# Cross-attention and a mixture of experts on one core: routing moved forward, copies laid out by rank, and the last sums split between TensorE and VectorE

## The chip, the cores and the metric

The kernel runs on one core of a Trainium2 chip. The time is the device time of the whole kernel in microseconds. The kernel before took 362.15 us as the median of 3 runs (361.63 to 363.35). Engines are called TensorE (PE), VectorE (DVE), ScalarE (ACT), GpSimd (POOL) and SyncE (SP).

## The reference

8 batches of 112 tokens with 256 features (896 tokens). First cross-attention with 16 heads over 375 context rows, then a mixture of 32 experts, of which each token uses 4, and a shared expert:

```
x = x + relu(attention(layernorm(x), ctx) @ wo.T + wo_b)
scores = softmax(xf @ gw + gb)              # xf = layernorm(x), 896 x 256; scores 896 x 32
keep the 4 best of 8 groups (by their two best experts), then the 4 best experts of these
y = sum over the 4 experts of weight * ((silu(xf@w1+b1) * (xf@w3+b3)) @ w2 + b2)
z = (silu(xf@sw1+sb1) * (xf@sw3+sb3)) @ sw2 + sb2
x = x + y + z
```

All of it is float32.

## The kernel before

The program has two blocks of instructions, `attention` and `experts`; at the end of the first all engines wait for each other.

**Attention** goes through 32 groups of four heads. At its end VectorE normalises the tokens of batches 0 to 6 (`normalise`, semaphore `xn_ok`), TensorE turns the last sums and projects batch 7, and VectorE normalises batch 7. TensorE fills waits with matmuls whose result nobody reads (`warm`, line 301).

**Routing** (start of `experts`): TensorE transposes the 896 normalised tokens (line 808), ScalarE and VectorE copy them to `xf`, TensorE makes the logits (line 816), and VectorE takes them through softmax, choice of groups and choice of experts (`choose`, `sel`). Every step of that row on VectorE waits for the one before (`chained`). Between the steps VectorE closes the shared expert's halves (`shared_h`, line 972), whose matmuls (`shared_up`, line 827) TensorE runs meanwhile. From `sel`, matmuls with `earlier` and `ones` count how many tokens chose an expert before each token and in all (lines 839 to 846). From these VectorE works out the place (slot) of each of the 3584 copies: each expert's copies lie together, in whole blocks of 128 rows. There are always 59 blocks; those that no expert needs come last.

**Scatter**: when `slots_ok` is given, GpSimd issues 32 indirect DMAs (line 794, `expert_rows<-normed,slots`) that write the rows of one batch each, rank 3 of all batches first, rank 0 last. Rank 0 of a token is its highest slot. SyncE loads block j (line 755, 128 KB) for j under 4 only when rank 3-j is scattered, so block 3 waits for all 32. Beside it VectorE makes a table of which expert owns each block, on one partition (lines 1062 to 1072), the weights of the copies (`gate`, lines 1075 to 1078), and adds the shared expert's result to `x2` (line 1082).

**Expert loop**: for each block TensorE transposes the rows (`turn_rows`, line 870), multiplies by the block's expert's w1 and w3 (`up`, line 878), transposes the product of silu and the other half (`turn_h`, line 887) and multiplies by w2 (`down`, line 893). VectorE adds biases (line 1106), multiplies (line 1112) and copies the result (`copy_y`, line 1088); ScalarE copies transposes and takes silu. GpSimd scatters each block's 128 results to `ys` in HBM (line 799, `expert_out<-hs,to`). Where each goes is worked out from marks read back from the blocks (`marks`, line 764; `results_go`, line 1095, called at j = 5), in time for the first of these scatters.

**Sums**: in `ys` the four copies of a token lie side by side. When all 59 scatters have landed, SyncE loads 8 batches of 448 KB (line 768, `b<-expert_out`), VectorE adds four weighted rows per batch to `x2` (line 1119), and SyncE writes each batch out (line 773). The buffer `rows` is the one of the biases, `b13`.

## Time and profile before

| What | Value |
|---|---|
| median of 3 runs | 362.15 us |
| profiled execution: its own time, its span | 361.01 us, 359.2 us |
| attention block | 0 to about 160 us |
| routing up to the first scatter | 160 to 186.8 us |
| 32 scatters up to block 3 in SBUF | 186.8 to 232.4 us |
| expert loop | up to 332.3 us |
| last result scatter landed | 337.1 us |
| loads, sums and stores | 337.1 to 359.2 us |
| busy share of PE, DVE, ACT, POOL | 81%, 62%, 42%, 51% |

The span is the time from the first to the last record of the profile; the time of the execution is a little longer. Busy shares are means over the whole span, so they say little of the stretches in which the engines wait for each other: those are read from the chain of waits and from the timeline.

### The profile page before, as it was taken

The numbers are of one execution on the slowest core, as the hardware profiler recorded it, in microseconds if no ns is written. First come the engines' busy times: TensorE is split into PE (matmuls) and PEld (weight loads), VectorE is DVE, ScalarE is ACT, GpSimd is POOL, SyncE is SP. The second block draws the span as 40 slices with busy tenths as digits, with TensorE's granted clock in tenths as the row PEclk, the third lists the DMA queues.
The fourth block names the chain that finished last, engine by engine and source line by source line (L and its number), as shares of the span: only waits on it lengthen the run. The fifth ranks groups of instructions, "written<-read, shape, count | busy, mean of one in ns | idle before, by whom it ended". The sixth has DMA issues, their size and how long they took to land.

```text
span 359.2 us, 7134 instructions
## 1 busy us (share of the span) xinstructions
PE 290.2 (81%) x2301; PEld 202.9 (56%) x2301; DVE 222.8 (62%) x708; ACT 150.9 (42%) x403; POOL 181.7 (51%) x188
## 2 busy tenths in 40 slices
PE   8999999999999999899898022199999999999000
PEld 3466666666666667656474011077778777776000
DVE  1678877767777778276969200065666666656097
ACT  1267666666566666515110000044545545544000
POOL 7266757565657566110027777307556555556200
PEclk9999999999999999999999555589999999999655
DMA  6795888959794900009502333385555455542495
GB/s 150 206 78 149 261 240 244 265 172 292 218 326 138 308 5 2 2 13 295 162 0 79 109 110 114 116 101 161 162 167 157 148 167 158 155 154 76 159 242 168
DMA packets 54013, 55.92 MB, mean 156 GB/s; under 512 B 18925, under 2 KB 45562, under 8 KB 53466
## 3 DMA queue, kind: packets, MB, share of 16 engines
q1 hardware_dynamic: 49610, 43.94, 45.6%
q0 software_dynamic: 4368, 11.52, 9.8%
q8 instruction: 21, 0.34, 0.4%
q14 instruction: 14, 0.11, 0.1%
HBM read 35.03 MB, written 20.41 MB: 154 GB/s over the span
## 4 chain that ended last, share of the span: by engine, by line
PE 29%; DVE 9%; POOL 9%; issue 4%; DMA 3%; ACT 0%; POOLq 0%; DVEq 0%; SPq 0%
PE ps L878 14%; POOL expert_rows L794 9%; PE ps L893 7%; DVE x L1119 4%; PE ps L870 3%; PE ps L887 2%; DMA b<-expert_out 1%; PE ps L816 1%; DMA expert_rows<-normed,slots 1%; DMA expert_out<-hs,to 1%; DMA xg<-expert_rows 1%; POOL expert_out L799 1%; PE ps L846 1%; PE ps L808 0%; PE ps L841 0%
## 5 line engine op out<-in xcount | busy, mean ns | idle before, releaser
L289 POOL TENSOR_SCALAR z<-z,zmax 112x375 f32<-112x375 f32 x64 | 78.7, 1241 | 52.7 <-DVE zmax L555 52.7
L799 POOL DMA_INDIRECT expert_out<-hs,to x59 | 56.6, 959 | 50.3 <-DVE hs L1088 35.2
L555 DVE CUSTOM_DVE_ANT_0 z<-ps,mask_sb 112x375 f32<-112x375 f32 x128 | 62.5, 546 | 28.8 <-PE ps L368 28.8
L483 ACT ACTIVATE pT<-ps 125x336 f32<-125x336 f32 x128 | 50.7, 448 | 38.1 <-PE ps L345 37.7
L878 PE MATMUL ps<-w,xgT 128*128 x236 | 64.1, 396 | 0.0
L345 PE MATMUL ps<-ident,z 112*125 112x112 f32 x384 | 56.6, 283 | 0.2 <-ACT pT L483 0.2
L345 PEld LDWEIGHTS ps<-ident,z 112*125 112x125 f32 x384 | 47.3, 188 | 15.4 <-ACT pT L483 7.3
L1106 DVE TENSOR_TENSOR hb<-ps,b 128x256 f32<-128x256 f32 x59 | 25.1, 425 | 49.1 <-PE ps L878 49.1
L794 POOL DMA_INDIRECT expert_rows<-normed,slots x32 | 32.4, 1014 | 35.1 <-DVE normed L1059 25.7
L878 PEld LDWEIGHTS ps<-w,xgT 128*128 128x128 f32 x236 | 43.5, 196 | 10.0 <-issue 1.8
L870 PE MATMUL ps<-ident,xg 128*128 128x128 f32 x118 | 24.0, 287 | 30.2 <-DMA xg<-expert_rows 30.2
L935 ACT COPY xgT<-ps 128x256 f32<-128x256 f32 x59 | 22.0, 373 | 46.4 <-PE ps L870 46.4
L893 PE MATMUL ps<-w2s,hs 128*128 x118 | 36.0, 387 | 0.0
L942 ACT COPY hs<-ps 128x128 f32<-128x128 f32 x59 | 15.7, 266 | 47.8 <-PE ps L887 47.8
L870 PEld LDWEIGHTS ps<-ident,xg 128*128 128x128 f32 x118 | 14.8, 146 | 33.2 <-DMA xg<-expert_rows 25.9
L1112 DVE TENSOR_TENSOR hh<-hb,sg 128x128 f32<-128x128 f32 x59 | 17.3, 293 | 19.5 <-ACT sg L947 17.0
L368 PE MATMUL ps<-kT,qT 32*112 32x375 f32 x256 | 28.8, 519 | 0.0
L381 PE MATMUL ps<-pT,vaug 125*32 125x112 f32 x768 | 25.0, 263 | 0.6 <-ACT pT L483 0.6
L1088 DVE COPY hs<-ps 128x256 f32<-128x256 f32 x59 | 24.5, 415 | 1.1 <-PE ps L893 0.6
L301 PE MATMUL ps<-ident 128*128 128x512 f32 x44 | 23.6, 669 | 1.6 <-POOL ident L256 1.6
L565 DVE TENSOR_SCALAR z<-z,zmax 112x375 f32<-112x375 f32 x32 | 23.7, 741 | 0.0
L1119 DVE SCALAR_TENSOR_TENSOR x<-b,gate,x 112x256 f32<-112x256 f32 x32 | 14.9, 484 | 8.9 <-DMA b<-expert_out 8.1
(159 smaller groups left out, 348.8 us busy)
## 6 DMA issues: line engine op xcount, KB each, us to landing
xg<-expert_rows SPq DMA_DIRECT2D x59, 128.0 KB, 2.3
expert_rows<-zero SPq DMA_DIRECT2D x14, 512.0 KB, 10.0
w2s<-in_L_ffn_w SPq DMA_DIRECT2D x2, 2048.0 KB, 9.6
b<-in_L_ffn_b SPq DMA_DIRECT2D x2, 2048.0 KB, 14.1
b<-expert_out SPq DMA_DIRECT2D x8, 448.0 KB, 9.3
ctx_sb<-in_ctx SPq DMA_DIRECT2D x8, 375.0 KB
mask_sb<-in_mask_Bx1xSxS_ff SPq DMA_DIRECT2D x8, 164.1 KB, 2.4
expert_out<-hs,to POOLq DMA_INDIRECT x59, 2.8
```

The lines of the kernel that those rows point to most:

```text
L289: pool.tensor_scalar(z[:, n % RING, :], z[:, n % RING, :], zmax[:, n % RING:n % RING + 1], None, ALU.subtract).then_inc(by_pool, 1)
L345: ins = nc.tensor.transpose(bank[0:KP, c * S:(c + 1) * S], z[:, n % RING, c * KP:(c + 1) * KP], ident[0:S, 0:S])
L368: nc.tensor.matmul(ps[0:S, S_BANK + j, 0:SK], qT[rows, b % 2, g // 2, g % 2, :], kT[rows, b % 2, g // 2, :], start=True, stop=True).then_i ...
L483: nc.scalar.activation(pT[:, n % RING, :], ps[0:KP, T_BANK + at % 2, 0:KT * S], ACT.Exp).then_inc(ring_read, 1)
L555: nc.vector.tensor_tensor_reduce(out=z[:, n % RING, :], in0=ps[0:S, S_BANK + j, 0:SK], in1=mask_sb[:, b % 2, :], scale=-1.0 if j in ACT_HE ...
L794: pool.indirect_dma_start(xs, bass.IndirectOffsetOnAxis(ap=slots[:, b, r:r + 1], axis=0), normed[:, b, :], None).then_inc(scattered[r], 16)
L799: pool.indirect_dma_start(ys, bass.IndirectOffsetOnAxis(ap=to[:, j:j + 1], axis=0), y_sb[:, j % 4, :], None).then_inc(y_sent[j % 4], 16)
L870: ins = nc.tensor.transpose(ps[:, T_BANKS[j % 2], k * P:(k + 1) * P], xg[:, j % 4, k * P:(k + 1) * P], ident[:])
L878: ins = nc.tensor.matmul(ps[:, U_BANKS[j % 2], 0:2 * INTER], xgT[:, j % 4, k, :], w13[:, k, bass.ds(owner_of(words, j), 1), :].rearrange(" ...
L893: nc.tensor.matmul(ps[:, Y_BANKS[j % 2], 0:D], hT[:, j % 4, :], w2s[:, bass.ds(owner_of(words, j), 1), :].rearrange("p o c -> p (o c)"), s ...
L1106: TT(hb[:, j % 2, :], ps[:, U_BANKS[j % 2], 0:2 * INTER], b13[:, bass.ds(owner_of(words, j), 1), :].rearrange("p o c -> p (o c)"), ALU.add ...
L1119: ins = nc.vector.scalar_tensor_tensor(x2[:, b, :], rows[:, TOPK * b + r, :], gate[:, b, r:r + 1], x2[:, b, :], ALU.mult, ALU.add)
```

## The change

- Transposes and logits of batches 0 to 6 go from `experts` to the end of `attention`, in place of four filling matmuls; ScalarE does the copies. Batch 7 follows in `experts`.
- `ones`, `earlier` and `sel` are of type float32r, so the counting matmuls are in that type.
- `shared_h` 0 and 1 come after `sel`, 2 and 3 after the slots; `shared_up` 2 and 3 come after the counting.
- The unused blocks come first instead of last (`free`). The table of owners is made with one block per partition and packed by one matmul. `gate` is made in the expert loop, one operation per block from j = 10.
- In the first three blocks `turn_rows` runs one block ahead instead of two, and `down(0)` stands ahead of `turn_rows(3)`.
- `ys` is ordered by rank and then token. Rank r of a token has at least r blocks behind it, so rank 3 is loaded when blocks up to 55 have landed, rank 2 up to 56, rank 1 up to 57, and rank 0 when all have.
- Batches 0 to 3 are summed by VectorE. For batches 4 to 7 ScalarE makes 16 diagonal matrices of the weights in the loop (from j = 23), and TensorE sums with them in PSUM, with filling matmuls between; ScalarE copies the sums to `x2`.

```diff
+    SHARES = (4, 2, 2, 2)
...
+        LOGITS = SUM_BANK
+        def route(pe, b):
+            for k in range(DK):
+                ins = nc.tensor.matmul(ps[0:S, LOGITS, b * E:(b + 1) * E], xf[:, k, b * S:(b + 1) * S],
+                                       gw_sb[:, k, :], start=(k == 0), stop=(k == DK - 1))
+            return ins
...
-                pool.iota(tag_i[:], [[TOPK * S, B]], base=0, channel_multiplier=TOPK).then_inc(places, 1)
+                pool.iota(tag_i[:], [[S, B]], base=0, channel_multiplier=1).then_inc(places, 1)
...
-                warm(4, S_BANK)
+                for c, own_batches in ((0, range(0, B // 2)), (1, range(B // 2, B - 1))):
+                    pe.wait_ge(xn_ok, own_batches.stop)
+                    for k in range(DK):
+                        for b in own_batches:
+                            at = (b - own_batches.start) * S
+                            ins = nc.tensor.transpose(ps[:, 2 * c + k, at:at + S], normed[:, b, k * P:(k + 1) * P], ident[0:S, 0:S])
+                        ins.then_inc(xT_full, 1)
+                pe.wait_ge(sums_ok, B)
+                for b in range(B - 1):
+                    if b in (0, B // 2):
+                        pe.wait_ge(xf_by_act, 2 if b == 0 else 4)
+                    route(pe, b)
...
+                for n, (lo, hi, k) in enumerate(((0, B // 2, 0), (0, B // 2, 1), (B // 2, B - 1, 0), (B // 2, B - 1, 1))):
+                    act.wait_ge(xT_full, n + 1)
+                    nc.scalar.copy(xf[:, k, lo * S:hi * S], ps[:, n, 0:(hi - lo) * S]).then_inc(xf_by_act, 1)
                 roots(B - 1, B, 4)
...
-            ones = sbe("ones", [S, P])
-            earlier = sbe("earlier", [S, S])
+            ones = sbe("ones", [S, P], F32R)
+            earlier = sbe("earlier", [S, S], F32R)
...
-            sel = sbe("sel", [S, B, E])
+            sel = sbe("sel", [S, B, E], F32R)
...
+            BY_DVE, BY_PE = range(0, B // 2), range(B // 2, B)
+            diag = xf[0:S].rearrange("p k c -> p (k c)").rearrange("p (n s) -> p n s", s=S)
...
+            GATES_AT = 10
+            DIAG_AT = GATES_AT + 3 * TOPK + 1
+            def next_rows(j):
+                if j < TOPK - 2:
+                    return range(j + 1, j + 2)
+                if j == TOPK - 2:
+                    return range(j + 1, j + 3)
+                return range(j + 2, min(j + 3, NBLK))
...
+                sp.wait_ge(hs_ok, 2 * NSH)
...
+                for r in reversed(range(TOPK)):
+                    for q in range(4):
+                        sp.wait_ge(y_sent[q], 16 * len(range(q, NBLK - r, 4)))
+                    wide = B // SHARES[r]
+                    for c in range(SHARES[r]):
+                        sp.dma_start(rows[:, r * B + c * wide:r * B + (c + 1) * wide, :],
+                                     ys[r * T + c * wide * S:r * T + (c + 1) * wide * S, :].rearrange("(b s) d -> s b d", s=S)
+                                     ).then_inc(rows_in[r][c], 16)
                 for b in range(B):
-                    sp.dma_start(rows[:, TOPK * b:TOPK * (b + 1), :].rearrange("s r d -> s (r d)"),
...
-                    sp.wait_ge(summed, b + 1)
+                    if b in BY_DVE:
+                        sp.wait_ge(summed, (TOPK - 1) * len(BY_DVE) + b + 1)
+                    else:
+                        sp.wait_ge(moved, b - BY_PE.start + 1)
                     sp.dma_start(out[b], x2[:, b, :]).then_inc(out_sent, 16)
...
+                b = B - 1
+                pe.wait_ge(xn_ok, B)
+                for k in range(DK):
+                    ins = nc.tensor.transpose(ps[:, 5, k * S:(k + 1) * S], normed[:, b, k * P:(k + 1) * P], ident[0:S, 0:S])
+                ins.then_inc(xT_full, 1)
+                pe.wait_ge(xf_by_act, 5)
+                route(pe, b).then_inc(logits_ok, 1)
...
-                for u in range(2 * NSH):
+                for u in range(2):
                     shared_up(u)
...
+                for u in range(2, 2 * NSH):
+                    shared_up(u)
...
+                    if b == 1:
+                        pe.wait_ge(owner_ok, 1)
+                        nc.tensor.matmul(ps[0:1, 6, P:P + NWORD], owner[:], pack[:], start=True, stop=True).then_inc(words_full, 1)
...
-                turn_rows(1)
...
-                    if j + 2 < NBLK:
-                        turn_rows(j + 2)
-                    if j >= 2:
+                    if j == TOPK - 2:
                         down(j - 2)
+                    for n in next_rows(j):
+                        turn_rows(n)
+                    if j >= 2 and j != TOPK - 2:
+                        down(j - 2)
+                def fill(n):
+                    for _ in range(n):
+                        nc.tensor.matmul(ps[:, H_BANK, :].rearrange("p (r c) -> p r c", c=P), ident[:],
+                                         ident[:].unsqueeze(1).to_broadcast([P, BANK // P, P]), start=True, stop=True)
+                pe.wait_ge(hT_ok, NBLK)
+                pe.wait_ge(xgT_ok, NBLK)
+                pe.wait_ge(biased, NBLK)
+                pe.wait_ge(diag_ok, len(BY_PE) * TOPK)
+                for b in BY_PE:
+                    nc.tensor.matmul(ps[0:S, b, 0:D], ident[0:S, 0:S], x2[:, b, :], start=True, stop=False)
+                fill(3)
+                for r in reversed(range(TOPK)):
+                    for b in BY_PE:
+                        pe.wait_ge(rows_in[r][b * SHARES[r] // B], 16)
+                        nc.tensor.matmul(ps[0:S, b, 0:D], diag[:, (b - BY_PE.start) * TOPK + r, :],
+                                         rows[:, r * B + b, :], start=False, stop=(r == 0)).then_inc(added, 1)
+                    if r > 0:
+                        fill(1)
...
+                act.wait_ge(xT_full, 5)
+                nc.scalar.copy(xf[:, :, (B - 1) * S:B * S], ps[:, 5, 0:DK * S].rearrange("p (k s) -> p k s", k=DK)).then_inc(xf_by_act, 1)
...
+                def turn_weights(n):
+                    act.wait_ge(gates_ok, n % TOPK + 1)
+                    nc.scalar.activation(diag[:, n, :], ident[0:S, 0:S], ACT.Copy,
+                                         scale=gate[:, BY_PE.start + n // TOPK, n % TOPK:n % TOPK + 1]).then_inc(diag_ok, 1)
...
+                    if DIAG_AT <= j < DIAG_AT + len(BY_PE) * TOPK:
+                        turn_weights(j - DIAG_AT)
+                for b in BY_PE:
+                    act.wait_ge(added, len(BY_PE) * (TOPK - 1) + b - BY_PE.start + 1)
+                    nc.scalar.copy(x2[:, b, :], ps[0:S, b, 0:D]).then_inc(moved, 1)
...
+                apart = mine[:].rearrange("s b e -> s (b e)")[0:4 * NWORD, 0:4 * NWORD].rearrange("p (n f) -> p n f", f=4)
+                chained(TT(apart, ident[0:4 * NWORD, 0:4 * NWORD].rearrange("p (n f) -> p n f", f=4),
+                           places5[0:4 * NWORD].unsqueeze(1).to_broadcast([4 * NWORD, NWORD, 4]), ALU.mult))
+                chained(nc.vector.tensor_reduce(pack[:], apart, AX.X, ALU.add))
...
-                shared_h(0)
...
-                shared_h(1)
...
-                TT(cw[:, :, 0:E], sc[:], sel[:], ALU.mult).then_inc(cw_ok, 1)
-                shared_h(2)
-                shared_h(3)
+                TT(cw[:, :, 0:E], sc[:], sel[:].bitcast(F32), ALU.mult).then_inc(cw_ok, 1)
+                shared_h(0)
+                shared_h(1)
...
+                chained(nc.vector.tensor_scalar(free[:], ends[:, E - 1:E], -1.0, float(NBLK), ALU.mult, ALU.add))
+                chained(nc.vector.tensor_scalar(ends[:], ends[:], free[:], None, ALU.add))
...
-                for lo in range(0, 4 * NWORD, STEP):
...
-                    chained(nc.vector.tensor_reduce(gate[:, :, r], mine[:], AX.X, ALU.add))
+                chained(nc.vector.tensor_scalar(passed[:], ends[0:4 * NWORD], slot[0:4 * NWORD, 0:1], None, ALU.is_le))
+                chained(nc.vector.tensor_reduce(owner[:], passed[:], AX.X, ALU.add))
+                nc.vector.tensor_scalar(owner[:], owner[:], float(E - 1), None, ALU.min).then_inc(owner_ok, 1)
+                shared_h(2)
+                shared_h(3)
+                dve.wait_ge(words_full, 1)
+                nc.vector.tensor_copy(word_i[:], ps[0:1, 6, P:P + NWORD]).then_inc(table_ok, 1)
+                dve.wait_ge(table_ok, 1)
+                words = [dve.value_load(word_i[0:1, n:n + 1], min_val=0, max_val=E ** 4 - 1) for n in range(NWORD)]
...
+                def weigh_copies(n):
+                    r = n // 3
+                    if n % 3 == 0:
+                        chained(TT(mine[:], key[:], best[:, :, r:r + 1].to_broadcast([S, B, E]), ALU.is_equal))
+                    elif n % 3 == 1:
+                        chained(TT(mine[:], mine[:], cw[:, :, 0:E], ALU.mult))
+                    else:
+                        nc.vector.tensor_reduce(gate[:, :, r], mine[:], AX.X, ALU.add).then_inc(gates_ok, 1)
...
+                    if GATES_AT <= j < GATES_AT + 3 * TOPK:
+                        weigh_copies(j - GATES_AT)
...
-                for b in range(B):
...
-                    ins.then_inc(summed, 1)
+                dve.wait_ge(acc_ok, B)
+                dve.wait_ge(gates_ok, TOPK)
+                for n, r in enumerate(reversed(range(TOPK))):
+                    for b in BY_DVE:
+                        dve.wait_ge(rows_in[r][b * SHARES[r] // B], 16)
+                        if n:
+                            dve.wait_ge(summed, (n - 1) * len(BY_DVE) + b + 1)
+                        nc.vector.scalar_tensor_tensor(x2[:, b, :], rows[:, r * B + b, :], gate[:, b, r:r + 1],
+                                                       x2[:, b, :], ALU.mult, ALU.add).then_inc(summed, 1)
```

## Rows read from the trace of the kernel before

**Rows 1.** Chain of waits, whole span: shares by line.

```profile
by line: PE ps L878 13.7%; POOL expert_rows L794 8.8%; PE ps L893 6.7%; DVE x L1119 4.2%; issue 3.7%; PE ps L870 3.5%; PE ps L887 2.1%; DMA b<-expert_out 1.1%; PE ps L816 0.9%; DMA expert_rows<-normed,slots 0.7%; DMA expert_out<-hs,to 0.7%;
```

**Rows 2.** Timeline, attention to experts: start, duration (us), what, idle before.

```profile
154.68 2.35 DVE L544 TENSOR_SCALAR normed<-x,mv,rstd 112x256 f32<-112x256 f32 x7
156.08 3.60 PE L301 MATMUL ps<-ident 128*128 128x512 f32 x8
...
159.94 0.31 POOL L778 MEMSET restart<- 112x256 f32 x1 [14.68 <-POOLq L1125]
...
160.59 0.54 ACT L919 COPY xf<-ps 128x448 f32<-128x448 f32 x1 [1.66 <-PE ps L808]
```

**Rows 3.** Chain of waits, routing: start, duration (us), what.

```profile
159.98 1.72 PE ps L808 x16
161.75 3.32 PE ps L816 x32
165.16 0.43 DVE lg L985
...
172.01 0.68 DVE hs L972
...
177.98 0.43 DVE sel L1023
...
182.68 0.40 DVE over L1045
...
186.76 1.85 POOL expert_rows L794
...
191.05 0.94 POOL expert_rows L794
```

**Rows 4.** Stretches of 0.5 us: busy time of each engine, clock, DMA.

```profile
198.00:198.50 0.50, 0.00 (x0) 0.00 (x0) 0.50 (x3) 0.00 (x0) 0.50 (x1) 0.62 0.72 224
...
235.50:236.00 0.50, 0.50 (x4) 0.42 (x3) 0.12 (x1) 0.43 (x2) 0.00 (x0) 0.84 1.22 67
```

**Rows 5.** Chain of waits, last scatter and load of block 3.

```profile
227.71 2.58 DMA expert_rows<-normed,slots
230.30 2.07 DMA xg<-expert_rows
```

**Rows 6.** Timeline of the loop, and one DMA issue (KB, us to landing).

```profile
232.51 0.38 SPq L764 DMA_DIRECT2D marks<-expert_rows  x1
...
239.82 0.40 DVE L1095 TENSOR_TENSOR own_copy<-marks,slot 128x236 f32<-128x236 f32 x1
...
241.66 0.98 POOL L799 DMA_INDIRECT expert_out<-hs,to  x1 [13.02 <-DVE to L1098]
...
252.96 0.42 DVE L1106 TENSOR_TENSOR hb<-ps,b 128x256 f32<-128x256 f32 x1 [0.48 <-PE ps L878]
...
marks<-expert_rows SPq DMA_DIRECT2D x1, 236.0 KB, 6.5
```

**Rows 7.** Chain of waits, end of the kernel.

```profile
330.78 0.96 POOL expert_out L799
...
334.57 2.39 DMA expert_out<-hs,to
337.11 4.02 DMA b<-expert_out
...
356.44 0.48 DVE x L1119
```

**Rows 8.** Stretches: PE, PEld, DVE, ACT, POOL busy; clock, DMA share, GB/s.

```profile
4.00:8.00 4.00, 4.00 (x7) 1.64 (x6) 0.58 (x2) 0.05 (x1) 3.44 (x3) 1.00 1.02 241
100.00:105.00 5.00, 4.58 (x54) 3.23 (x54) 4.00 (x13) 3.58 (x9) 2.62 (x3) 1.00 1.04 331
...
339.00:343.00 4.00, 0.00 (x0) 0.00 (x0) 1.74 (x4) 0.00 (x0) 0.00 (x0) 0.50 0.96 278
343.00:350.00 7.00, 0.00 (x0) 0.00 (x0) 6.64 (x15) 0.00 (x0) 0.00 (x0) 0.50 1.04 238
```

More of the change, by code:

```diff
@@ L9 @@
 F32 = mybir.dt.float32
+F32R = mybir.dt.float32r
 U32 = mybir.dt.uint32
@@ L156, in xattn_moe_kernel @@
         xn_ok = sem("xn_ok")
+        xT_full = sem("xT_full")
+        xf_by_act = sem("xf_by_act")
+        logits_ok = sem("logits_ok")
         zero_ok = sem("zero_ok")
@@ L672, in xattn_moe_kernel @@
         y_sent = [sem(f"y_sent{q}") for q in range(4)]
-        rows_in = [sem(f"rows_in{b}") for b in range(B)]
+        gates_ok = sem("gates_ok")
+        diag_ok = sem("diag_ok")
+        added = sem("added")
+        moved = sem("moved")
+        rows_in = [[sem(f"rows_in{r}_{c}") for c in range(SHARES[r])] for r in range(TOPK)]
         summed = sem("summed")
@@ L711, in experts @@
             ends = sbe("ends", [P, E])
+            free = sbe("free", [P, 1])
             base1 = sbe("base1", [P, E])
@@ L735, in experts @@
             rows = b13[0:S]
+            ones1 = above[:].rearrange("s b e -> s (b e)")[:, 0:P]
+            earlier1 = above[:].rearrange("s b e -> s (b e)")[:, P:P + S]
             sil = xg[:].rearrange("p q d -> p (q d)")[:, 0:2 * CT].rearrange("p (u c) -> p u c", u=2)
@@ L780, in _ @@
                 pool.memset(cw[:], 1.0).then_inc(const_ok, 1)
-                pool.memset(ones[:], 1.0).then_inc(ones_ok2, 1)
+                pool.memset(ones1[:], 1.0).then_inc(ones_ok2, 1)
                 pool.wait_ge(const_ok, 3)
@@ L785, in _ @@
                 pool.wait_ge(ones_ok2, 1)
-                pool.affine_select(out=earlier[:], in_=ones[:, 0:S], compare_op=ALU.is_gt, fill=0.0, base=0,
+                pool.affine_select(out=earlier1[:], in_=ones1[:, 0:S], compare_op=ALU.is_gt, fill=0.0, base=0,
                                    pattern=[[1, S]], channel_multiplier=-1).then_inc(ones_ok2, 1)
+                pool.tensor_copy(ones[:], ones1[:]).then_inc(ones_ok2, 1)
+                pool.wait_ge(ones_ok2, 3)
+                pool.tensor_copy(earlier[:], earlier1[:]).then_inc(ones_ok2, 1)
                 pool.wait_ge(slots_ok, 2)
@@ L962, in over_e @@
                     return ap.unsqueeze(2).to_broadcast(shape)
-                for c in range(NCH):
-                    dve.wait_ge(xT_full, DK * c + 2)
-                    nc.vector.tensor_copy(xf[:, 1, c * CT:(c + 1) * CT], ps[:, DK * c + 1, 0:CT]).then_inc(xf_by_dve, 1)
                 def shared_h(u):
@@ L1053, in _ @@
                            base1[0:S].unsqueeze(1).to_broadcast([S, B, E]), ALU.add))
-                chained(TT(key[:], key[:], sel[:], ALU.mult))
+                chained(TT(key[:], key[:], sel[:].bitcast(F32), ALU.mult))
                 for b in range(B):
@@ L1059, in _ @@
                 nc.vector.tensor_scalar(normed[:, :, D:D + TOPK], best[:, :, 0:TOPK], -1.0, None, ALU.add).then_inc(slots_ok, 1)
-                for lo in range(0, 4 * NWORD, STEP):
-                    some = slice(lo, min(lo + STEP, 4 * NWORD))
-                    n = some.stop - lo
-                    passed = xf[0:1].rearrange("p k c -> p (k c)")[:, 0:n * E].rearrange("p (j e) -> p j e", e=E)
-                    chained(TT(passed, ends[0:1].unsqueeze(1).to_broadcast([1, n, E]),
-                               count1[0:1, some].unsqueeze(2).to_broadcast([1, n, E]), ALU.is_lt))
-                    chained(nc.vector.tensor_reduce(owner[:].rearrange("p n f -> p (n f)")[:, some], passed, AX.X, ALU.add))
-                chained(nc.vector.scalar_tensor_tensor(owner[:], owner[:], float(E - 1),
-                                                       places5[:].unsqueeze(1).to_broadcast([1, NWORD, 4]), ALU.min, ALU.mult))
-                chained(nc.vector.tensor_reduce(word[:], owner[:], AX.X, ALU.add))
-                nc.vector.tensor_copy(word_i[:], word[:]).then_inc(table_ok, 1)
-                for r in range(TOPK):
-                    chained(TT(mine[:], key[:], best[:, :, r:r + 1].to_broadcast([S, B, E]), ALU.is_equal))
-                    chained(TT(mine[:], mine[:], cw[:, :, 0:E], ALU.mult))
-                    chained(nc.vector.tensor_reduce(gate[:, :, r], mine[:], AX.X, ALU.add))
+                chained(nc.vector.tensor_scalar(passed[:], ends[0:4 * NWORD], slot[0:4 * NWORD, 0:1], None, ALU.is_le))
[7 more added lines that the diff above has]
+                words = [dve.value_load(word_i[0:1, n:n + 1], min_val=0, max_val=E ** 4 - 1) for n in range(NWORD)]
                 for b in range(B):
@@ L1112, in _ @@
                         TT(hh[:, j % 2, :], hb[:, j % 2, INTER:2 * INTER], sg[:, j % 2, :], ALU.mult).then_inc(h_ok, 1)
-                for b in range(B):
-                    dve.wait_ge(rows_in[b], 16)
-                    if b == 0:
-                        dve.wait_ge(acc_ok, B)
-                    for r in range(TOPK):
-                        ins = nc.vector.scalar_tensor_tensor(x2[:, b, :], rows[:, TOPK * b + r, :], gate[:, b, r:r + 1],
-                                                             x2[:, b, :], ALU.mult, ALU.add)
-                        if r < TOPK - 1:
-                            chained(ins)
-                    ins.then_inc(summed, 1)
+                dve.wait_ge(acc_ok, B)
[7 more added lines that the diff above has]
+                                                       x2[:, b, :], ALU.mult, ALU.add).then_inc(summed, 1)
         with ExitStack() as own_tiles:
```

61 lines of the change are left out of this document (20 added, 41 removed).

## The prediction, made before the changed kernel was run

> **What bounds the kernel now.** I read the page first: no engine bounds all of it. The chain of waits by line [rows 1] then splits the end of the kernel: the expert loop is a chain of TensorE lines (878, 893, 870, 887), but POOL's scatter of the rows (794) holds 8.8% and VectorE's last sums (1119) 4.2%. In order of time there are four links. Routing runs from 159.94, when both blocks' engines have met, to the first scatter at 186.76 [rows 2, 3], nearly all of it single VectorE steps behind each other. The scatter: 32 indirect DMAs up to 227.71, 2.58 to landing, 2.07 for block 3's load [rows 5]; blocks 0 to 2 are worked in its shadow. The loop, about 1.67 us a block. The end: last result scatter at 334.57, landed 337.11, first sum four us later, last sum at 356.44, span 359.2 [rows 7]. So a change helps only if it brings forward the first scatter, shortens the 32, or shortens what follows the last blocks. I call T3 the landing of the last row scatter (230.30) and TL that of the last result scatter (337.11).
>
> **Routing.** *Logits.* Normalised rows of batches 0 to 6 are complete at 154.68 + 2.35 = 157.03, while TensorE runs filling matmuls from 156.08 to 159.68 [rows 2]. In their place: transposes at 1.72/16 = 0.107 each (14: 1.5), four ScalarE copies of about 0.54 or less, one behind the other, and 28 of 32 logit matmul instructions at 3.32/32 = 0.104 [rows 2, 3]. First transposes 156.1, copies 156.7 to 158.8, logits of batches 0 to 3 at 158.0 to 159.65, of 4 to 6 to 160.95. The four filling matmuls hid this up to 159.68; beyond that it delays the meeting of the engines by 1.3, to 161.25. Then batch 7 alone: transposes and copy about 0.75, four matmul instructions 0.4, hand-overs 0.4, so VectorE begins line 985 at 162.8 instead of 165.16 [rows 3]: 2.35 less. VectorE's preparation, now with two more steps, ends about 162.7 and just fits. POOL's two extra copies lie in the same time. Bounds: 1.0 (the ScalarE copies late) to 3.5.
>
> *shared_h 0 and 1* stood in the chain as 172.01 and its twin; each delayed the next step by 0.6 [rows 3]. Off: 1.2.
>
> *Counting.* From the end of sel (178.41) to line 1045 (182.68) are 4.27 [rows 3] for 32 matmul instructions at the full clock. No row shows the price of float32r; a float32 product here is two instructions, so I count one in its place, 16 instead of 32 for lines 841 and 846. But TensorE is now idle before them: two shared_up end near 169, sel comes at 174.9. In the trace the granted clock fell from 2.4 to 1.2 GHz at 198.2, after TensorE had gone idle at 196.5, and came back to 2.4 at 235.6, over 3 us after work had begun again [rows 4]. So half as many at twice the duration: nothing gained, bounds 2.0 less (they stay at 2.4 GHz) and 2.0 more (float32r is no cheaper by instruction, all at 1.2 GHz). VectorE has shared_h 0 and 1 in this time.
>
> *free* adds two chained steps of about 0.2: 0.4 more. The first scatter comes 2.35 + 1.2 + 0 - 0.4 = 3.1 earlier, at 183.6.
>
> **Scatter.** The first two took 1.85, while VectorE made the table in four operations of over a microsecond on one partition; from 191.05 on they took 0.94 [rows 3]. The weights' operations beside the next five made them about 1.05. Both go away: the table is three small operations, and the weights move to the loop. 1.8 + 0.5 = 2.3 off. Lower bound 0.5, if the first two were slow because they were first. The Trainium skill ("SBUF — State Buffer", "Who interferes with whom") says that GpSimd and VectorE lock a port pair against each other when VectorE has two SBUF inputs while GpSimd reads SBUF. By that rule the weights' and the compare operations cost what they cost, and shared_h 2 and 3 and the additions to x2, with one input in PSUM, cost nothing: the same 2.3. The 0.94 of scatters beside the additions agrees.
>
> TensorE's shared work now partly follows the counting: two shared_up (6), eight batches (13), done by about 201; block 3 is needed after 224.9. Hidden. T3 moves 3.1 + 2.3 = 5.4, to 224.9.
>
> **Start of the loop.** After T3 TensorE had up(2), turn_h(1) and down(0) still to do; now they are done before. That is worth some 2 us: up(3) could start at T3 + 3.5 instead of T3 + 5.6. But results_go at j = 5 needs the marks, issued at T3 + 2.2 and landing 6.5 later, T3 + 8.7. Its first operation ran at 239.82 = T3 + 9.5, and hb(5) waited for its four operations [rows 6]. So the marks' landing becomes the bound after 0.8 us: I take 0.6 less. Bounds 0 and 2.
>
> **In the loop.** 12 operations of 0.42 on VectorE, one a block, each ahead of hb. VectorE sat idle 0.48 before hb [rows 6]: they fit barely; with 0.05 for the wait each, I allow 0.3 in all. If that cover is missed by half an operation in each block: 12 x 0.2 = 2.4. The 16 diagonals on ScalarE, about 0.3 each, stand behind silu, where ScalarE next waits 0.7 or more for turn_h: nothing. If they were late, 16 x 0.3 = 4.8. Empty blocks first instead of last changes no count; the last blocks' results now go to scattered rows like those of the middle: nothing. POOL's loop scatters have slack.
>
> **The end.** Before, from TL to the end of the span: 359.2 - 337.11 = 22.1, VectorE's 32 operations running without a pause once the first load was there. Now: the result scatters run 1.27 apart at the end (330.78 to 334.57 for three) [rows 7], so block 55 has landed about TL - 3.5, and rank 3 starts then; the others follow as their blocks land, and DMA always has work. To move: 3.67 MB and the last three scatters' 0.39, 4.06 MB. The rate: 278 GB/s beside VectorE alone, 238 with stores in the traffic (packets of 4 KB); rows of 1 KB on 112 partitions moved at 241 early in the kernel, those on 128 with stores at 331 [rows 8]. I take 270, near the row without stores, since the stores now come last: 15.0. With 2 for the first and last latency: TL - 3.5 + 17.0 = TL + 13.5. Behind the last landing: TensorE's two products 0.9 (its filling and products should keep it at 2.4 GHz), ScalarE's copy 0.4, hand-overs 0.4, and the last store as now, 359.2 - 356.92 = 2.3 [rows 7]: 4.0. VectorE's half (16 operations, 7.8) runs in step with the loads and is done before. End TL + 17.5 instead of TL + 22.1: 4.6 less. By 241 it is 2.7 less, by 331 it is 7.3 less.
>
> The Trainium skill ("DMA: Bandwidth & Descriptors", "Anatomy of one DMA") gives 2.0 us and then 436 GB/s for a DMA; that would be an estimate of 9.3 for the 4.06 MB, and a total some 6 us below mine. The rows of the tail contradict it: its DMA share was 0.96 to 1.04 at 238 to 278 GB/s.
>
> **Sum.** 5.4 + 0.6 - 0.3 + 4.6 = 10.3. Profiled execution 361.01 - 10.3 = 350.7; the median of the runs lies 1.14 above that execution, so 351.8.
>
> **Rivals.**
> 1. *The forecast*: routing 3, scatter 2, end 4 to 5. 346.5 to 356. Chance 0.66.
> 2. *The scatters were slow for being first, and the loads run at 241*: gain 3.1 + 0.5 + 0.6 - 0.3 + 2.7 = 6.6, time 355.6. For: the very first two, at 241 GB/s a row of like shape. Against: later ones also slowed under VectorE's weights. 0.14.
> 3. *Counting at 2.4 GHz or cheap at 1.2, loads at 300 or more*: 2 more and 2.7 more, 347.1. For: 331 at 100 us. Against: 238 in the tail itself; an idle gap of 6 before counting. 0.13.
> 4. *The loop's pace breaks*: VectorE's and ScalarE's added operations come late (2.4 + 4.8) : gain 3.4, 358.8. For: the 0.48 is thin. Against: ScalarE's slack. 0.04.
> 5. *Slower*: the loads of 1 KB packets into the buffer go at under half the rate. The front's 5.7 less is lost when the tail grows by 5.7: TL + 27.8 = -3.5 + 2 + 4.0 + 4.06/rate, a rate of 160 GB/s. At 120 the tail ends at TL + 36.3, 14.2 later, and the time is 370.7. Against: no stretch with 1 KB packets and a full DMA share was that slow. 0.03. That the sums could stay on VectorE's pace is excluded by the code, which gives it half.
>
> Less than 0.5% (1.8 us) is about what a measurement of this kernel can tell from no change. Faster takes rivals 1 to 4 but for the upper edge of 4 and of misses that add up: 0.95; within 0.02; slower 0.03. The range, 346.0 to 356.6, holds the forecast's span and most of rivals 2 and 3; the rest is some 0.15.
>
> **What would show it.** In the profile after: the engines meet at 161.2 and line 985's successor starts near 162.8; the first scatter near 183.6 and of 0.94 to 1.0; a granted clock of half in the counting; the last row scatter landed near 225; marks bind results_go; blocks still 1.67 apart from j = 10 to 38; loads of rank 3 issued 3.5 before the last landing, the last load landed 13.5 after it, and 4 from there to the end. A first scatter later than 185, scatters of 1.85 again, a wait of TensorE for hh in j = 10 to 21, or loads that end 16 or more after TL would make the forecast wrong.

## The result, and the profile after

The changed kernel took 351.58 us (median of 4 runs, 351.42 to 351.92) against 362.02 for the kernel before (4 runs), a ratio of 0.972 with a 95% interval of 0.968 to 0.975. Run again later (run 9), beside 11 runs of the kernel before, it took 352.79 against 361.41, a ratio of 0.977 (0.975 to 0.978). So the gain is 8.6 to 10.4 us. The two profiled executions stand 9.09 apart (361.01 and 351.92, the span of the latter 350.1), and the terms below are of these two. The executions of the changed kernel differ among themselves by 0.5 us here and by 2.4 in run 9, so a term of a few tenths is a reading of two traces and no proof by itself; the logits, `shared_h` and the order ahead of block 3 were not tried alone.

Chain of waits of the changed kernel, routing (start, duration, what), to be laid beside [rows 2, 3]; logits are L1087, the counting L897 to L904:

```profile
162.97 0.44 DVE lg L1087
...
174.62 0.44 DVE sel L1125
...
175.10 0.56 PE ps L897
175.65 1.15 PE ps L899 x7
176.80 1.72 PE ps L904 x8
...
178.54 0.40 DVE over L1146
...
179.81 0.16 DVE free L1152
...
183.08 1.16 POOL expert_rows L859
```

Of the page, the busy shares of the engines and the chain by line; before they were 81%, 62%, 42% and 51%, and [rows 1]:

```profile
PE 308.0 (88%) x2331; PEld 212.3 (61%) x2331; DVE 209.9 (60%) x691; ACT 158.1 (45%) x426; POOL 179.8 (51%) x190
...
PE ps L941 13%; POOL expert_rows L859 8%; PE ps L956 6%; PE ps L933 3%; DMA b<-expert_out 3%; PE ps L950 2%; DMA expert_out<-hs,to 1%; PE ps L996 1%; DMA expert_rows<-normed,slots 1%; DMA xg<-expert_rows 1%; POOL expert_out L864 1%; DVE hb L1214 1%; PE ps L904 0%; DVE best L1108 0%; ACT sg L1030 0%
```

VectorE's last sums (4.2% before) are gone from the chain; transfers of results (`b<-expert_out`, 3%) and TensorE's products with the diagonal matrices (L996, 1%) stand there instead. The first scatter starts 3.7 earlier than before (186.76). The chain of waits again, from the last row scatter into the loop ([rows 5, 6]). L941 is `up`, here of block 3; `hh` is the product behind it on VectorE, and `own_copy` the first of the four operations that need the marks:

```profile
221.92 2.56 DMA expert_rows<-normed,slots
224.50 2.04 DMA xg<-expert_rows
...
226.58 1.29 PE ps L933 x4
...
228.01 2.07 PE ps L941 x4
...
233.48 0.29 DVE hh L1220
233.77 0.33 DVE own_copy L1201
```

Stretches (PE, PEld, DVE, ACT, POOL busy; granted clock, DMA share, GB/s), first around the counting, then in the tail ([rows 4, 8]):

```profile
172.50:173.00 0.50, 0.00 (x0) 0.00 (x0) 0.47 (x3) 0.00 (x0) 0.00 (x0) 0.72 1.08 295
...
175.00:178.00 3.00, 2.90 (x15) 2.90 (x15) 1.65 (x4) 0.00 (x0) 0.00 (x0) 0.50 0.68 194
...
230.50:231.00 0.50, 0.50 (x4) 0.47 (x3) 0.50 (x2) 0.34 (x2) 0.00 (x0) 0.75 1.52 82
...
330.00:332.00 2.00, 1.19 (x3) 0.19 (x1) 0.00 (x0) 0.00 (x0) 0.07 (x1) 1.00 1.01 336
...
336.00:338.00 2.00, 1.24 (x4) 0.38 (x2) 1.32 (x4) 0.00 (x0) 0.00 (x0) 1.00 1.12 238
```

Chain of waits at the end ([rows 7]); the last result scatter is issued at 329.12 (334.57 before):

```profile
327.86 4.79 DMA expert_out<-hs,to
...
333.04 9.47 DMA b<-expert_out
342.56 1.98 PE ps L996 x8
...
345.40 1.83 PE ps L996 x8
347.25 0.37 ACT x L1048
```

Laid side by side, the 9.1 us are (the landing of the last row scatter itself took 2.6 in both):

| stretch | before | after | gain | forecast |
|---|---|---|---|---|
| first scatter starts | 186.76 | 183.08 | 3.7 | 3.1 |
| first to last row scatter | 40.95 | 38.84 | 2.1 | 2.3 |
| landing of the last to first result scatter | 11.36 | 11.05 | 0.3 | 0.6 |
| first to last result scatter | 92.91 | 93.59 | -0.7 | -0.3 |
| last result scatter issued to end of span | 24.63 | 20.98 | 3.7 | 4.6 |

### The profile page after: what moved, and what is told of

It reads as the page before. It is cut to its first block, busy times and chain, and to the rows that moved or that the text cites. A ratio compares the mean times of both kernels' runs of the same rounds, so it can differ in the third digit from the quotient of the medians.

```text
span 350.1 us, 7231 instructions
## 1 busy us (share of the span) xinstructions
PE 308.0 (88%) x2331; PEld 212.3 (61%) x2331; DVE 209.9 (60%) x691; ACT 158.1 (45%) x426; POOL 179.8 (51%) x190
## 4 chain that ended last, share of the span: by engine, by line
PE 27%; POOL 9%; DVE 6%; DMA 5%; issue 4%; ACT 1%; DVEq 0%; SPq 0%; POOLq 0%
PE ps L941 13%; POOL expert_rows L859 8%; PE ps L956 6%; PE ps L933 3%; DMA b<-expert_out 3%; PE ps L950 2%; DMA expert_out<-hs,to 1%; PE ps L996 1%; DMA expert_rows<-normed,slots 1%; DMA xg<-expert_rows 1%; POOL expert_out L864 1%; DVE hb L1214 1%; PE ps L904 0%; DVE best L1108 0%; ACT sg L1030 0%
## 5 line engine op out<-in xcount | busy, mean ns | idle before, releaser
L941 PE MATMUL ps<-w,xgT 128*128 x236 | 65.5, 402 | 3.0 <-ACT xgT L1020 2.8
L941 PEld LDWEIGHTS ps<-w,xgT 128*128 128x128 f32 x236 | 43.8, 198 | 14.4 <-issue 6.4
L859 POOL DMA_INDIRECT expert_rows<-normed,slots x32 | 30.3, 948 | 29.5 <-DVE normed L1163 20.0
L1030 ACT ACTIVATE sg<-hb 128x128 f32<-128x128 f32 x59 | 18.3, 310 | 6.9 <-DVE hb L1214 5.6
L316 PE MATMUL ps<-ident 128*128 128x512 f32 x36 | 19.3, 663 | 1.6 <-POOL ident L271 1.6
```

The costliest lines, as they stand in the source:

```text
L859: pool.indirect_dma_start(xs, bass.IndirectOffsetOnAxis(ap=slots[:, b, r:r + 1], axis=0), normed[:, b, :], None).then_inc(scattered[r], 16)
L941: ins = nc.tensor.matmul(ps[:, U_BANKS[j % 2], 0:2 * INTER], xgT[:, j % 4, k, :], w13[:, k, bass.ds(owner_of(words, j), 1), :].rearrange(" ...
```

## The experiments

All are edits of the changed kernel. The theory is the sum above; the first four runs test its terms for counting, scatter and end. Ratios are to the kernel before, measured beside each run.

**1. Counting in float32.** `ones`, `earlier` and `sel` declared without F32R.

> The changed kernel with ones, earlier and sel in float32 again, nothing else. In its trace the counting took from the end of sel at 175.05 to line 1146's start at 178.54, 3.5 us, at a granted clock of 0.50, with 16 matmul instructions; the kernel before took 4.3 with 32 at 1.00. Theory A (the type halves the instructions, and the cost goes by instruction and clock): 32 instructions at half clock, 6.5 to 7.5 us of counting, the first scatter at about 186.5 instead of 183.1, time 354.5 to 355.5. Rival B (the type hardly matters, the counting is bound by something that the clock does not set): within 0.5 of the changed kernel's 351.6.

Measured: 357.39 us, ratio 0.987 (0.982 to 0.991). Its chain:

```profile
177.00 1.20 PE ps L897 x2
178.19 3.33 PE ps L899 x14
181.53 3.43 PE ps L904 x16
184.98 0.40 DVE over L1146
```

Twice the instructions at the same clock of 0.50: 8.0 us against 3.5. The type is worth 4.5 us here; moved behind an idle TensorE without it, the counting would have cost 3.7 more than in the kernel before. (`sel` was also 1.9 late in this execution, so the median, 2 us above what was expected, holds more than the type.)

**2. The clock kept for the counting.** Five filling matmuls ahead of the wait for `sel`:

```diff
+                for _ in range(5):
+                    nc.tensor.matmul(ps[:, 7, :].rearrange("p (r c) -> p r c", c=P), ident[:],
+                                     ident[:].unsqueeze(1).to_broadcast([P, BANK // P, P]), start=True, stop=True)
                 pe.wait_ge(sel_ok, 1)
```

> The changed kernel with five filling matmuls (4.3 us at full clock) between the second shared_up and the wait for sel. Theory A (the half clock costs the counting its time): granted clock 1.00 through the counting, counting 2.0 to 2.5 us instead of 3.5, first scatter 1.0 to 1.5 earlier, time 350.1 to 350.6. Rival B (float32r is bound by weight loads and hand-overs at either clock): the clock is 1.00 and the counting still takes over 3.2, time 351.3 to 351.8.

Measured: 351.02 us, ratio 0.969 (0.966 to 0.973). Chain:

```profile
175.00 0.38 PE ps L899
175.38 0.61 PE ps L901 x7
175.99 0.91 PE ps L906 x8
176.92 0.40 DVE over L1148
```

From the end of `sel` the counting takes 2.0 instead of 3.5, and the last row scatter lands 1.5 earlier (222.98). But the first result scatter comes only 0.6 earlier, at 234.90. Something at the loop's start takes 0.9 back. `up(3)` began at 226.59 and ran 2.07 at half clock, as in the changed kernel, and the full clock came back between 230.5 and 231 in both, so the work that now began 1.4 earlier ran longer at the half one. The marks had come earlier with the scatters. That spoke for the clock and was tested in run 10. The median is 0.5 above the range of theory A, and its interval overlaps that of the changed kernel: by the times alone, these fillers do nothing that can be told.

**3. All ranks loaded late.** Each rank's loads wait for all 59 blocks: `range(q, NBLK - r, 4)` becomes `range(q, NBLK, 4)`.

> The changed kernel in which every rank's load waits for all 59 result scatters, as in the kernel before; the sums stay split. Theory A (the end is bound by bytes over a full DMA, so starting three scatters earlier is what the change gains there): loads begin at about 331.5, and the last scatters land sooner without them beside, 15.5 to 16 us of moving and 4.5 behind it: end 1.5 to 3.5 later, time 353.2 to 355. Rival B (the early loads only slow the last scatters, whose landing took 4.8 instead of 2.4, so nothing is gained): within 0.5 of 351.6. Rival C (the split of the sums was worth nothing, all came from the early start): above 355.5.

Measured: 355.96 us, ratio 0.984 (0.980 to 0.988), above the range of theory A and by its time in that of C. The chain of waits:

```profile
330.11 2.41 DMA expert_out<-hs,to
```

From this issue of the last result scatter to the end are 24.0, against 21.0 in the changed kernel and 24.6 before. So the early loads are worth 3.0 of the 3.7, and layout and split together 0.6; the other 1.0 by which this execution is longer lies ahead of the tail. In the changed kernel the last two scatters land in 4.79 (above) and 5.5, here the last in 2.41: beside the early loads the landings are slower.

**4. Long VectorE steps beside the scatter.** Ahead of the table: three compares with two SBUF inputs, three reductions and three copies of 1x1024, behind `slots_ok`. Their output is not used.

> The changed kernel with nine added VectorE steps right behind the slots, on one partition of 1024 elements: three compares of two inputs in SBUF, three reductions and three copies in SBUF. Their results are not used. Theory A (VectorE's steps with SBUF operands hold up the scatters): scatters beside compares take 1.5 to 1.9 instead of 0.94; what kind of step does it, the durations beside reductions and copies tell; time 1 to 4 later, 352.5 to 355.5. Rival B (the first scatters were slow for being the first): only the very first is over 1.0, time within 0.5 of 351.6.

Measured: 355.54 us, ratio 0.984 (0.979 to 0.988). The timeline (start, duration, engine, line, operation):

```profile
183.13 3.70 DVE L1167 TENSOR_TENSOR zero<-ends,count 1x1024 f32<-1x1024 f32 x3
183.52 1.86 POOL L859 DMA_INDIRECT expert_rows<-normed,slots  x1 [20.44 <-DVE normed L1163]
185.68 1.97 POOL L859 DMA_INDIRECT expert_rows<-normed,slots  x1 [0.30 <-issue]
186.87 3.69 DVE L1170 TENSOR_REDUCE mine<-zero 1x32 f32<-1x1024 f32 x3
187.96 0.94 POOL L859 DMA_INDIRECT expert_rows<-normed,slots  x1 [0.30 <-issue]
...
190.59 2.11 DVE L1172 COPY zero<-zero 1x1024 f32<-1x1024 f32 x3
191.70 1.13 POOL L859 DMA_INDIRECT expert_rows<-normed,slots  x1 [0.30 <-issue]
```

Only the scatters beside the compares double. The one beside reductions of the same size costs nothing more, the one beside copies 0.2. Rival 2 ("slow for being first") falls: without the compares the first takes 1.16. The Trainium skill ("SBUF — State Buffer", "Who interferes with whom") gives this for operations with two SBUF inputs; the trace agrees with 1.86 and 1.97 against 0.94. From the first to the last row scatter are 40.7, 1.9 more than in the changed kernel; the rest of the 3.3 by which this execution is longer lies mostly at the loop's start (the first result scatter 12.9 behind the landing instead of 11.05) and its cause was not looked for.

**5 to 8** are to tell the remaining terms apart: the split (5), the clock at block 3 (6), the weights in the loop (7) and the order at the end (8). They ran on another chip than runs 1 to 4, where the kernel before took 365.7.

5 gives all batches to VectorE and leaves out TensorE's sums with their fillers and waits:

```diff
-            BY_DVE, BY_PE = range(0, B // 2), range(B // 2, B)
+            BY_DVE, BY_PE = range(0, B), range(B, B)
```

6 puts three filling matmuls ahead of the transposes of block 3:

```diff
                     for n in next_rows(j):
+                        if n == TOPK - 1:
+                            for _ in range(3):
+                                nc.tensor.matmul(ps[:, H_BANK, :].rearrange("p (r c) -> p r c", c=P), ident[:],
+                                                 ident[:].unsqueeze(1).to_broadcast([P, BANK // P, P]), start=True, stop=True)
                         turn_rows(n)
```

7 takes the calls of `weigh_copies` out of the loop and puts this ahead of it:

```diff
+                for n in range(3 * TOPK):
+                    if n % 3 == 0 and n:
+                        dve.wait_ge(gates_ok, n // 3)
+                    weigh_copies(n)
```

8 loads TensorE's batches of rank 0 first, stores batches 4 to 7 first, and leaves out the filler between TensorE's last two ranks:

```diff
-                    for c in range(SHARES[r]):
+                    for c in ((2, 3, 0, 1) if r == 0 else range(SHARES[r])):
...
-                for b in range(B):
+                for b in [*BY_PE, *BY_DVE]:
...
-                    if r > 0:
+                    if r > 1:
                         fill(1)
```

> The changed kernel with the sums of all eight batches on VectorE, 32 operations of about 0.48, 15.5 us in all, and no product, filling or copy for them on TensorE and ScalarE; the ranks are loaded early as in the change. Theory A (the end is bound by the bytes of the loads at about 240 GB/s, and VectorE's 3.9 us a rank keeps step with 3.8 us of loading a rank): the last load lands as before, two to four operations and the store follow, time 350.5 to 352.5, so the split gives nothing. Rival B (VectorE falls behind: the first operation at 332.4, 32 of them without a pause to 347.9, and a rank's waits on top): 353 to 355.

> The changed kernel with three filling matmuls ahead of turn_rows(3), in the 5 us in which TensorE waits for the last scatter. In its trace up(3) ran in 2.07 at half clock, 3.5 after the last row scatter had landed, and the first result scatter came 11.05 after that landing, where the kernel before had 11.36. Theory A (the clock takes back what the earlier blocks give): granted clock 1.00 from turn_rows(3), the first result scatter 9.5 to 10.3 after the landing, the last one 1 to 2 earlier, time 349.8 to 350.9. Rival B (the marks bound it, as I predicted: they land 8.7 after it): up(3) is fast and results_go waits for the marks, the first result scatter stays within 0.4 of 11.05 - 0.4, time within 0.5 of 351.6.

> The changed kernel with the twelve operations for gate in one row ahead of the loop (as the kernel before had them, beside the scatters) instead of one a block from j = 10. Theory A (in the loop they cost 0.7 to 0.9, since VectorE's pause before hb is 0.45 to 0.68 and an operation with its wait 0.47; beside the scatters they cost four compares and four products of two SBUF inputs, 0.1 each): spacings of the result scatters at j = 10 to 21 as in the kernel before, last row scatter 0.5 to 0.9 later, time 351.2 to 352.0. Rival B (nothing in the loop is due to them): the spacings of 2.06 and 1.99 stay.

> The changed kernel in which rank 0's shares for TensorE (batches 4 to 7) are loaded ahead of VectorE's, their results are stored first, and no filling matmul stands between the products of ranks 1 and 0. In the changed kernel's trace the last load landed about 345.6 and the last product ended 347.2. Theory A (after the last landing TensorE's path, two to four products and a ScalarE copy, is 0.7 to 1.0 longer than VectorE's two operations): the end comes 0.7 to 1.2 earlier, time 350.3 to 351.0. Rival B (only the bytes count): within 0.4 of 351.6.

Measured: 368.72, 371.04, 370.96 and 369.17, ratios 1.008 (1.004 to 1.012), 1.015 (1.009 to 1.021), 1.014 (1.008 to 1.021) and 1.010 (1.004 to 1.016). All are 14 to 19 above the upper ends of what was expected, each with another edit; the kernel before is slower there by only 4 (365.7 against 362.0). Their row scatters still end as in the changed kernel (the last one is issued at 221.7 to 222.0, in run 5 at 223.6 behind a `sel` that was 1.6 late), but the first result scatter comes at 248.7 to 251.2 instead of 235.5. The loss lies on VectorE behind the table of owners. The chain of waits of run 7:

```profile
196.73 0.46 DVEq L1175
197.19 0.70 issue
197.89 0.70 DVEq L1175
198.61 0.69 issue
...
211.25 0.76 DVE x L1180 x2
...
214.69 13.37 another core or an unknown queue
228.08 1.42 DVE x L1180 x4
```

Line 1175 reads the 15 words into registers. Up to 197 its steps take 0.2 to 0.5, and then they come 0.70 apart for 14 us, and after four of the additions (L1180) come 13.4 of waiting for something that the profile cannot name. TensorE waits for the additions from 201.6 until 229.5. In the changed kernel the same stretch took 9.55 (table at 189.56, additions at 199.27), hidden beside the scatters. From the issue of the last result scatter to the end, these four show 21.0, 21.7, 20.6 and 21.7. So run 8's order does not show a shorter end either, though no twin on this chip stands beside it; it was not repeated, and its question stays open.

**9. The changed kernel again**, to tell edits from circumstances.

> The changed kernel itself, word for word. In the last four runs (every edit in another place) VectorE took 20 to 21 us from the table of owners to its first addition to x2 (9.6 in the first five profiles), its register instructions coming 0.70 us apart, and all four ended 14 to 18 us later than their edits explain. Theory A: this is a matter of the chip or of where the program's instructions lie on it, not of the edits: if this call runs under the same conditions, the changed kernel too takes 366 to 369 with the 20 us in its chain; if not, 351 to 352 with 9.6, and the two sums on another chip stay without a twin here. Theory B: the edits caused it: 351 to 352 here, and the all-on-VectorE kernel of this same call at 366 or more.

Measured: 352.79 us (351.10 to 353.45), with 9.9 on VectorE. Run 11 is the same kernel as run 5 and took 352.73 instead of 368.72, 16.0 less, of which the kernel before shows 4.3 (361.41 against 365.7). So run 5's loss is not its edit's; runs 6 to 8 show the same pattern, and the edits of 6 (with six fillers for three) and 7 were used again in runs 10 and 12 without it. What it comes from (the chip, or where the instructions lay) is open, and so is whether the changed kernel would lose it there too.

**10. The clock kept twice.** Run 2's fillers, and those of run 6 with `range(6)` for `range(3)`.

> The changed kernel with five filling matmuls ahead of the counting and six ahead of the transposes of block 3 (TensorE is idle there from 221.5 to 226.6). Theory: the clock at the loop's start took back what an earlier last scatter brings. Then the row scatters land at 223.0, up(3) runs in 1.1 us instead of 2.07, the first result scatter is at 233.6 or earlier (235.53 before), the last at 326 (329.12), and the median is 348.5. Rival: the marks' landing (6.5 after its issue) holds the first result scatter and the loop behind it: first result scatter at 234.7 and a median of 351.

Measured: 349.84 us (349.57 to 350.37), ratio 0.968 (0.966 to 0.969), apart from run 9's 0.977 (0.975 to 0.978): 3 us faster than the changed kernel. Its chain after the last row scatter (sent at 220.13, landed at 222.69):

```profile
224.83 6.54 DMA marks<-expert_rows
231.39 0.42 DVE own_copy L1207
```

and TensorE's timeline there:

```profile
219.23 5.64 PE L980 MATMUL ps<-ident 128*128 128x512 f32 x12
...
225.95 1.12 PE L943 MATMUL ps<-w,xgT 128*128 x4 [0.16 <-issue]
...
232.30 0.44 PE L935 MATMUL ps<-ident,xg 128*128 128x128 f32 x2 [1.54 <-DMA xg<-expert_rows]
```

`up(3)` takes 1.12 instead of 2.07. The first result scatter comes 10.5 behind the landing (11.3 in run 9), and now the marks bind: theory and rival were both right, one behind the other, which leaves the last scatter at 326.97 and not at 326. TensorE too waits here, 1.54, for the rows of the next block. The profiled executions stand only 0.7 apart (350.37, the slowest of run 10, and 351.10, the fastest of run 9): run 10's has won 1.9 by the last result scatter and loses 1.2 behind it, where that scatter took 8.1 to land instead of 5.1. So the 3 us rest on the medians; the traces show 1.5 for the counting and 0.75 for block 3 (`sel` was 0.3 later in run 10).

**11. All sums on VectorE, again.**

> The changed kernel with all eight batches summed by VectorE; ScalarE's diagonals and TensorE's sums are left out. From the issue of the last result scatter to the end of the span, the changed kernel took 21.0 us, and this kernel 21.0 in the run before. Theory A: the early loads set the end, the split between engines adds nothing: tail of 20.5 to 21.5 and the median of g1 within 0.8 us. Theory B (what I forecast by): VectorE's 16 operations more, 0.48 each, come on top: tail of 24 or more, 3 us later than g1.

Measured: 352.73 us (350.72 to 353.13), run 9 has 352.79. Stretches of the tail, run 11:

```profile
338.00:340.00 2.00, 0.00 (x0) 0.00 (x0) 1.93 (x6) 0.00 (x0) 0.00 (x0) 0.50 1.13 268
```

and run 9, in the same columns, and from its chain of waits:

```profile
334.00:336.00 2.00, 2.00 (x6) 1.42 (x6) 0.07 (x1) 0.00 (x0) 0.00 (x0) 0.50 1.12 251
...
333.68 3.76 PE ps L996 x8
```

VectorE alone is busy nearly all the time and keeps just behind the loads: 19.8 us from the issue of the last result scatter to the end, against 20.4 in run 9 (theory A had 20.5 to 21.5, theory B 24 or more). In run 9 TensorE's eight products of rank 3 took 3.76, since the clock had fallen in the 2.7 us that they waited for the first load (1.98 at the full clock in the changed kernel's first trace), and from them to the end the chain is TensorE's. The 16 diagonals, the fillers and the split give nothing that the median shows. This run also tells what the diagonals cost in the loop, since it has none: from the first to the last result scatter are 93.69, against 93.72 in run 9, so nothing.

**12. As 10, with the weights ahead of the loop.**

> As g2_clock_kept_twice, and the 12 operations for the weights stand ahead of the loop instead of in blocks 10 to 21. Theory A: in the loop they cost 0.4 to 0.7 us, ahead of it 0.5, since the eight of them with two SBUF inputs run beside row scatters: the same median as g2 within 0.5 us, with 0.5 less from the first to the last result scatter (93.6 in the changed kernel) and up to 0.5 more for the row scatters. Rival: ahead of the loop they are free (VectorE is idle there): 0.7 us less than g2.

Measured: 349.31 us (347.63 to 350.67), not to be told from run 10. First to last result scatter 93.4 (93.7 in run 10), four row scatters at 0.96 to 1.07 instead of 0.94: 0.3 won, 0.4 lost. The rival (0.7 less than run 10) falls with that. Without the weights in the loop, the spacings of the 8th to the 18th result scatter are those of the kernel before to 0.01, but two wide ones behind them stay, 2.21 and 2.08 (2.15 and 2.08 in run 7, 2.06 and 1.99 in the changed kernel, 1.85 and 1.74 before). Neither the weights nor, by run 11, the diagonals make these; what does is open. (The profiled execution of run 12, the slowest of its six, had `sel` 2.3 later than that of run 10. So only stretches are compared.)

Runs 10 and 12 are the fastest versions; the intervals of both lie below the changed kernel's.

## Why the prediction was right, point by point

T3 is, as in the prediction, the landing of the last row scatter.

- **Logits, shared_h, free.** 2.19, 1.17 and 0.45 against 2.35, 1.2 and 0.4. The engines met at 161.27 (161.25 forecast).
- **Counting.** The clock fell as forecast, from the full to the half one at 172.5 to 173, TensorE idle since 170.5. I set half as many instructions at twice the duration, no gain; it was 3.49 instead of 4.27. The 16 instructions took 0.21 each, and the 32 before 0.13, so 1.6 times and not twice. This gain of 0.8 is more than the whole surplus of the first scatter (0.6).
- **Scatter.** 2.1 against 2.3: the first still took 1.16. Run 4 showed the cause, the compares. (The weights slowed four scatters and not five.)
- **Start of the loop.** The step failed in its cause, and by 0.3 in size. I had `up(3)` start at T3 + 3.5 (it did) and named the marks as the bound, with no word on the clock. TensorE had been idle for 5 us and `up(3)` ran at half clock. The marks landed at 233.1 (issued at 226.6, 6.5 to land), T3 + 8.6 as forecast, but `own_copy` came only 0.6 later, behind an `hh` of a block that the half clock had made late. Run 10 shows both: 0.75 from the clock, and then the marks.
- **In the loop.** I allowed 0.3 for the twelve operations; the loop lost 0.7. In the view of waits from 238 to 322 us (line, what it waited for: us in total, times, longest), which stands below this list, `hb` (the addition of the biases) comes late behind VectorE's own added operation. Run 12 gives 0.3 of it back, which is the price that I had set, and run 11 shows that the diagonals cost nothing, as forecast. The other 0.4 are mostly in the two wide spacings; I had no term for them, and their cause is open.
- **The end.** Forecast 4.6, found 3.7. Two sizes were off. The loads took 17.9 from the first issue (327.84) to the last landing (345.7), where I had 17.0: 336 GB/s in the first two us, but 237 to 246 from 334 to 344, where I took 270. And 4.4 followed behind the last landing, where I had 4.0; the loads began 0.3 sooner than forecast. The last two scatters landed in 4.8 and 5.5 instead of 2.4, so rank 0 was asked for later, but a price of that is not shown: the DMA share stayed at 1.1, and run 12, which asked for rank 0 only 8.7 behind the last issue, has the shortest end (19.7). That VectorE's and TensorE's halves would keep step was right. But I counted on the split to make it possible, and wrote in run 11's expectation that VectorE alone would take 3 more; it took none. So the start of the loads is the gain (3.0 by run 3), and the split has no part in it that shows. The estimate of 9.3 in the prediction goes by figures that the Trainium skill ("DMA: Bandwidth & Descriptors", "Anatomy of one DMA") gives for DMAs issued by GpSimd, and these loads are issued by SyncE.
- **Sum.** 0.6 more than forecast at the first scatter, and 0.2, 0.3, 0.4 and 0.9 less behind it. By the profiled executions the gain is 9.1, not 10.3, and the execution after took 351.92, not 350.7. I had added 1.14 to come to the median, since the median before lay above its profiled execution; the median after lies 0.34 below its own. These two misses, 1.2 and 1.5, cancel, and that the median came within 0.3 us of the forecast is luck. The repeat in run 9 has a gain of 8.6.
- **Rivals.** 2 fell by run 4 for the scatter, though its slow loads (241) came near the truth at the end. Of 3, the cheap counting is true by 0.8, the fast loads are not. 4 is not borne out: the loop lost 0.4 more than forecast, but neither the weights nor the diagonals made that. 5 needed under 160 GB/s; the loads moved 237 and more up to 344.

```profile
DVE hb L1214 <- DVE mine L1194: 1.4, 4, 0.6
```

## What to carry to other kernels

When work is moved away from in front of a TensorE step on the critical chain, price that step at the clock that an idle TensorE leaves behind, and fill the gap with matmuls that end before the step's data come (here 3 us by the medians, 2.3 by the stretches). Where the end of a kernel is bound by transfers, start the loads as soon as their rows are safe (3.0 here) before splitting the arithmetic (nothing here). And of VectorE's work beside indirect DMAs, move the operations with two SBUF inputs first.

## What the runs showed of the hardware that was not expected

- VectorE's register instructions can come 0.70 us apart for 14 us (run 7), where the same ones before 197 in that trace take 0.2 to 0.5; the changed kernel and its all-on-VectorE variant were 2.3 and 2.4% faster than the kernel before on one chip, and that same variant 0.8% slower on another.
- Indirect scatters of 128 rows land in 2.4 without bulk loads (run 3) and in 4.8 and 5.5 beside loads that fill the DMA queues (end of the changed kernel); the last one took 5.1 in run 9, 7.2 in run 11 and 8.1 in run 10.
- 16 float32r products of the counting take 3.4 at half clock and 1.9 at the full one; the 32 of float32 take 8.0 at half clock.
- The granted clock fell to half in a wait of 2.7 us ahead of the sums in one execution (run 9) and stayed at full through one of 3.2 in another (the changed kernel's first trace).
